# A two-layer token tower on one core: the 32 early gathers of the second combine each wait for two further tiles of the expert loop

## The reference, cut to what matters

```python
v1, i1 = top_k(x @ g1, 2)                 # 2 of 8 groups for each token
v2, i2 = top_k(einsum('td,gde->tge', x, g2), 2)   # 2 of 8 experts in each group
h = relu(einsum('td,gedh->tgeh', x, W1) + b1)     # 128 -> 256
y = einsum('tgeh,gehd->tged', h, W2) + b2         # 256 -> 128
out = sum over the 4 picks of softmax weight * y
```

## Time and profile before

| | us |
|---|---|
| time, median of 3 runs | 1164.05 (1163.82 to 1165.67) |
| the profiled execution: span from first to last instruction | 1254.4 |
| the profiled span less the median | 90.35 |
| GpSimd busy (POOL), in the profiled execution | 536.2 |
| VectorE busy (DVE) | 748.9 |
| TensorE busy (PE) | 737.2 |

### The profile page before, as it was taken

One profiled execution on the slowest core, in us unless ns is written; L12 is line 12 of the kernel. 1 busy time (PEld: TensorE's weight loads), 2 busy tenths in 40 slices (PEclk: granted clock), 3 DMA queues, 4 the chain that ended last, 5 costly groups with the idle time before them and its releaser, 6 DMA issues.

```text
span 1254.4 us, 16064 instructions
## 1 busy us (share of the span) xinstructions
PE 737.2 (59%) x4622; PEld 585.6 (47%) x4622; DVE 748.9 (60%) x2175; ACT 406.2 (32%) x1123; POOL 536.2 (43%) x562
## 2 busy tenths in 40 slices
PE   0205966669999237878597413577777894452000
PEld 0205355559999214434255401366666894442000
DVE  6896174856666318788776799555555552275222
ACT  2274151524444133433102306533333462220000
POOL 8853000245450645563100005756666306347664
PEclk9657975559999656676665655589999997665555
DMA  2390049502221266657500404033333222112221
GB/s 67 113 388 1 1 143 320 173 24 68 71 72 42 58 119 127 142 124 137 94 0 1 129 0 138 23 83 85 88 86 88 77 64 66 53 43 77 63 54 52
DMA packets 113503, 111.45 MB, mean 89 GB/s; under 512 B 15891, under 2 KB 99922, under 8 KB 113170
## 3 DMA queue, kind: packets, MB, share of 16 engines
q1 hardware_dynamic: 100172, 83.36, 24.5%
q0 software_dynamic: 13248, 27.06, 8.4%
HBM read 76.08 MB, written 34.26 MB: 88 GB/s over the span
## 4 chain that ended last, share of the span: by engine, by line
PE 46%; DVE 30%; issue 10%; another core or an unknown queue 6%; ACT 3%; DMA 2%; POOL 1%; SPq 1%; DVEq 0%; ACTq 0%; POOLq 0%
PE ps L639 13%; PE ps L646 12%; DVE wide L1330 6%; DVE h L1309 5%; PE ps L1896 4%; PE ps L634 2%; DVE bnst L964 2%; DVE wide L1208 2%; PE ps L2066 2%; PE ps L2107 2%; PE ps L2156 1%; ACT wide L1694 1%; PE ps L2046 1%; DVE mv L967 1%
## 5 line engine op out<-in xcount | busy, mean ns | idle before, releaser
L871 POOL DMA_INDIRECT wide<-xrows,holder x188 | 180.1, 958 | 137.5 <-PE ps L634 91.1
L639 PE MATMUL ps<-wide 128*128 (+1 forms) x1324 | 205.9, 288 | 42.6 <-issue 25.4
L646 PE MATMUL ps<-big,wide 128*128 x1312 | 196.2, 282 | 40.3 <-issue 21.7
L639 PEld LDWEIGHTS ps<-wide 128*128 128x128 f32 x1324 | 174.7, 198 | 56.2 <-issue 53.3
L646 PEld LDWEIGHTS ps<-big,wide 128*128 128x128 f32 x1312 | 171.8, 196 | 43.7 <-issue 43.6
L512 DVE TENSOR_SCALAR wide<-ps,wide 128x128 f32<-128x128 f32 x331 | 109.2, 348 | 129.5 <-PE ps L639 78.6
L1330 DVE TENSOR_REDUCE wide<-ps 125x3 f32<-125x1500 f32 (+1 forms) x96 | 143.7, 1540 | 46.4 <-PE ps L1896 44.4
L606 ACT ACTIVATE wide<-ps,wide 128x128 f32<-128x128 f32 x331 | 114.0, 366 | 169.8 <-PE ps L639 132.9
L1896 PE MATMUL ps<-big 97*125 97x500 bf16 x256 | 105.4, 548 | 40.3 <-DVE wide L1330 33.0
L949 POOL DMA_INDIRECT wide<-results,place x96 | 95.8, 998 | 68.2 <-SPq L494 26.8
L862 POOL TENSOR_SCALAR wide<-tileno,sm 125x128 f16<-125x128 f16 x64 | 40.8, 644 | 168.4 <-DVE sm L1195 143.9
(11 more groups left out here) (384 smaller groups left out, 1197.2 us busy)
## 6 DMA issues: line engine op xcount, KB each, us to landing
results<-wide SPq DMA_DIRECT2D x129, 128.0 KB, 1.8
big<-kappa SPq DMA_DIRECT2D x8, 1750.0 KB, 21.4
big<-parts SPq DMA_DIRECT2D x96, 125.0 KB
big<-in_L_ffn_W_dram SPq DMA_DIRECT2D x10, 1024.0 KB, 9.6
big<-in_L_ffn_W_dram SPq DMA_DIRECT2D x64, 128.0 KB, 2.7
parts<-wide SPq DMA_DIRECT2D x24, 250.0 KB
xrows<-wide SPq DMA_DIRECT2D x2, 1792.0 KB
wide<-xrows,holder POOLq DMA_INDIRECT x188
```

Source lines behind the costliest of these rows:

```text
L639: last = t.matmul(ps[:, (2 if k < c.HC // 2 else 4) + u % 2, 128 * k:128 * k + 128], ring.w1[u % U][:, 128 * k:128 * k + 128], turned, sta ...
L646: last = t.matmul(ps[:, 6 + u % 2, 0:D], ring.hid[u % 2][:, 128 * k:128 * k + 128], w[:, D * k:D * k + D], start=k == 0, stop=k == c.HC - 1)
L871: gp.indirect_dma_start(ring.rows[j % RING], None, xrows[:, :], bass.IndirectOffsetOnAxis(ap=holder[:, j:j + 1], axis=0)).then_inc(S(f"row ...
```

## The change

One wait is added in the loop over the 32 early gathers, ahead of each. Gather number n = 8b + i (0 to 31) now waits until `f1_w1_ready` has reached 160 + 2n, but at most 193:

```diff
@@ -881,6 +881,7 @@
                     pool.wait_ge(S(q + "w1_ready"), LOWER_AT + 6)
                     for b in range(EARLY):
                         for i, (k, t) in enumerate(picks_of(b)[0:8]):
+                            pool.wait_ge(S(q + "w1_ready"), min(LOWER_AT + 2 * RING + 2 * (8 * b + i), c.tiles + 5))
                             gp.indirect_dma_start(early_rows[8 * b + i], None, results[f][:, :],
                                                   bass.IndirectOffsetOnAxis(ap=place[f][:, k, t:t + 1], axis=0)
                                                   ).then_inc(S(f"early{b}"), 16)
```

## The result

The changed kernel takes 1170.15 us (median of 5 runs, 1166.66 to 1171.31) against 1163.82 for the kernel before (5 runs, 1161.38 to 1165.67): ratio 1.0047, 95% interval 1.0032 to 1.0062, or 5.5 us more. (The ratio is the recorded one and goes by all runs; the two medians are 6.3 apart.) Ratios leave out runs in a slower state with a lower granted clock, which met one run of the kernel before and one of the change, both on chip 11. Its profiled execution took 1171.3 us, which lies among the other four, with a span of 1169.1. So no 90 us are added here, and the span did not fall to 1234 as I had forecast but to 1169.

The account below looks back on a forecast made before the run. The prediction took the program's end as bound by GpSimd's queue of gathers. Terms 4.5 (queue delay) + 0 (waits) + 0.4 (slowed loop) = 4.9 us on 1164.05 gave 1169.0; 8-in-10 range 1162 to 1174.5, main case 1166.4 to 1174.5.

Parts of the forecast that it names:

- (1): Early gathers: the first five added waits cost nothing, as the semaphore at 167 already stands above thresholds 160 to 166.
- (2): Early gathers 5 to 16 are paced by the expert loop, two tiles taking 2.04 us against 1.255 for a gather.
- (3): Early gathers 17 to 31 wait for the last weight copy; gather 17 and the queue behind it come 4.5 us later.
- (4): The added wait instructions on GpSimd themselves: taken as nothing; 0.1 us for each of 15 would be 1.5.
- (5): Late gathers: 12 us of spare before the change, but GpSimd then waits for nobody, so nothing hides the 4.5 us.
- (6): Expert loop: paced gathers slow it by 4.8 us in the profile, 0.4 us without the profiler, the real part.
- I take the stall as mostly the profiler's own: Expert loop beside early gathers: its 38 us loss lies mostly in the profile, not in a run without the profiler.
- my list: Unexplained time beside gathers: loop 38, row stage 35, late gathers 10, first combine 14; sum 97 to 98 against 90.35 us.
- The frame without the stall: Unprofiled timeline assumed for the program's end: the loop's last copy at 1066.9, the results in at 1069.2.
- Rival A: Expert loop: the stall beside back-to-back gathers is real and pacing cures it; 20.9 us faster, 1143 us, chance 0.17.
- The sign of being wrong: Profile and time of the changed kernel: a time falling along with the span would say the stall is real.
- The forecast for the profile: Changed kernel's profile: the span falls by about 20 us to some 1234 while the time rises.

Follow-up runs that it names:

- one tile: Kernel before with each early gather waiting for one further tile instead of the change's two; 1164.7 us, ratio 0.9994 to the kernel before.
- the doses: Kernel before with early gathers waiting for two further tiles each, three each, or all for the last weight copy: 1170.15, 1178.06 and 1191.83 us.
- the slow kernel: Kernel before with VectorE's three wide products at the loop's end cut into 8 pieces each, on chip 11: 1262.79 us, ratio 1.0014.
- the clean one: Kernel before, unedited, timed and profiled anew, without the stall: 1164.44 us, span 1164.1, ratio 0.9978 to itself.
- hold alone: Kernel before with early gathers 0 to 16 as they were and 17 to 31 waiting for the last weight copy; 1170.24 us, ratio 1.0032.

## Why the prediction was right, and where its reasons were not

The time (1169.0 forecast, 1170.15 measured) and the mechanism, a queue on GpSimd that is late by what the loop holds it back, were right on the chips where it was timed. Step by step:

- **(1) The first waits cost nothing.** Right: 26 copies were left at the first gather, and gathers 0 to 8 kept 1.25 us.
- **(2) Pacing.** Right: 1.8 to 2.2 us between gathers 9 to 16, with VectorE L504 as the releaser.
- **(3) Gather 17, +4.5 us.** Measured 27.0 us behind the first gather (1016.34 - 989.33) against 21.4 (1011.27 - 989.89): +5.6. Of the 1.1 us that it lacks, 0.3 are the loop (the last copy starts 26.2 us behind the first gather, not 25.9) and 0.3 the copy itself, whose end and not its start gives the signal. The other 0.5 the step overlooked: gather 16, with its threshold of 192, goes at 1015.09 and takes its own 1.25 us, so that 17 comes half a microsecond behind the signal, not with it. At the first late gather 5.2 are left, since the five gathers beside VectorE's sums and products are stretched a little less.
- **(4) The waits.** Zero within the error, as taken: one tile adds 32 of them, ratio 0.9994 (0.9976 to 1.0013).
- **(5) No cover left.** Right, and shown by the doses: 5, 12.4 and 26 us of delay in the queue are 5.5, 12.2 and 26.9 us of time.
- **(6) 0.4 us for a slowed loop.** Nothing: 25.1 us for 26 copies with and without spacing, and with no gather beside them. The 0.4 was made of a share of a stall that these chips don't have; it stands in for part of the 1.1 us of step 3, by luck.

**The step that failed** is the one ahead of the sum: "I take the stall as mostly the profiler's own". The profiler makes no such stall: profiled executions without it differ from their reported time by about 2 us (1169.1 and 1171.3; 1164.1 and 1165.83), and so does one with it (1259.3 and 1261.01). The 90 us go with the chip, or with the condition that it was in: on chip 11, 16 of 17 runs of the kernel before take 1256 to 1265 us. It is not TensorE's clock, whose mean grant was 0.719 in the slow kernel's profile there and 0.725 in that of the kernel before on chip 12. Other work on the same chip was not ruled out, and chip 11 was used in one round only. The first profile against the clean one of the same kernel, with the row gathers of the second expert layer from the first profile,

```profile
L871 POOL DMA_INDIRECT wide<-xrows,holder x125: 938/945/1070, 800.9 to 991.0; - x125
```

gives: start of the row gathers 800.9 against 787.6 (13.3 us); row gathers 190.1 against 156.6 (33.5); to the first early gather 50.0 against 45.7 (4.3); from there to the last copy 64.1 against 25.9 (38.2); to the first late gather 2.5 against 18.7 (-16.2); late gathers 136.2 against 119.2 (17.0). Together 90.1 of the 90.3 between 1254.4 and 1164.1. Of the 13.3, 10.2 lie in the first combine's 64 gathers (155.6 us against 145.4). The other 3.1 and the 4.3, some 7 us in all, lie outside the places of my list.

That list (38, 35, 10, 14) had the first two sizes about right and the others not (17.0 and 10.2), and the owner wrong. Its sum of 98, so near to 90, is a coincidence: it counts the loop's 38 in full, though GpSimd's own queue hides 16.2 of them, as the clean kernel waits 18.7 us from its last copy to its first late gather anyway. The prediction's step 5 has this spare itself, as 12 us; taken off the 98 it leaves 86, less than the 90, and nothing for a run without the stall.

The frame without the stall fitted the chips that timed the kernels only because they were unlike the profiled one. So the number is right by a sound step 1 to 5 and by luck in what stands ahead of them. That the first profile comes from a chip like chip 11 is inferred from its pattern, not recorded.

**Rival A** ("the stall is real, and pacing cures it", 20.9 us faster) is what happens on chip 11: 24 us faster, interval 22 to 27. Its price had been worked out from the same rows, and its loop's end came out: 30.5 us behind the first gather (1073.6 - 1043.09), where it has 30.7. What the prediction held against it, the sum of 98 against 90, was no argument, as shown. The sign of being wrong that it names, a time that falls along with the span, was seen there: 1236.69 us at a span of 1234.7.

The rule of the Trainium skill ("NOTIFIC — the notification-queue block", measured rates), that a record costs the engine no cycle, is not tested, since no run is known to be without records. What the runs show is that recording does not make 90 us, and the gap that I held against the rule came from somewhere else. The gap of 6.2 us in "Runtime: NRT & Kernel Launch" (the launch sequence) is not seen: here the span is about 2 us *below* the reported time. But the span runs from the first to the last instruction and need not be the total of which the page speaks.

The forecast for the profile (a span of some 1234) came true on chip 11 alone (1234.7). It failed in the profile beside the result.

**What stays open:** what differs on chip 11, and why ScalarE and VectorE start so late there while gathers run. In the first profile both start their halves at 1084.20, 15.5 us after the last matmul recorded ahead of them (1068.66); the traces show no more. Open is also what cures the stall: the rate of one gather per two tiles, or any wait that ties the gathers to the loop. The hold alone and one tile would tell, on chip 11.

## What to carry to other kernels

When a profile's span and the timed median differ by per cents, compare a second profile, and times from the chip that was profiled, before explaining anything in the first: stalls may go with the chip, and a change can then lose on one and win on another (+0.47% and -1.93% here). The queue here was busy up to the end and paid each delay in full, so a wait put in front of a part of it cost the time by which its turn came late; a wait whose threshold was passed by then was free. Where a run-ahead queue has to be tied to its neighbours, a loose threshold costs less than a tight one; which one still holds off the stall was not found here.

## What the runs showed of the hardware that was not expected

- The same program takes 1164 to 1166 us on four chips and 1260.8 us on a fifth. In the profiles at hand all but some 7 of the 90 us lie beside gathers issued by GpSimd. That no chip but this one is like it, or that it stays so, is not shown.
- An indirect gather of 125 rows costs GpSimd 1.196 us and lands 3.3 us after issue; one of 128 rows 0.944 and 2.5.
- A gather on GpSimd beside VectorE's products of 2,048 columns with two operands in SBUF takes up to 2.75 us instead of 0.94; beside pieces of 256 columns at most 1.17 us. In the profile of the kernel before on chip 12 the three stretched gathers end at 1023.28, 1025.48 and 1027.80, each 0.8 to 0.9 us after the end of the product that ran when it started (1022.4, 1024.66 and 1026.98), so they seem to wait for that end and then take about their usual time. The page "SBUF — State Buffer" of the Trainium skill, in its section on the two separate sides, speaks of a port pair that the two share and hold for a whole instruction; the rows agree with that.
